# Routing of the second expert layer done batch by batch inside attention, into one DRAM bucket per expert

## The reference, cut to what matters

```
x = x + 0.5 * ffn(layernorm(x))
x = x + attention(layernorm(x))            # 16 heads of 8, causal softmax
x = x + 0.5 * ffn(layernorm(x))            # the same weights again

def ffn(inputs):                           # 8 experts, 128 -> 512 -> 128
    num = einsum('bsd,ed->bse', inputs, waff)
    aff = num / (|inputs| * |waff| + 1e-9)
    cap = floor(S * sigmoid(aff.mean() - threshold)), kept in 4..S   # mean over ALL tokens
    tcr = one_hot(argmax(softmax(aff)))    # each token's one expert
    ranks = argsort(argsort(-aff, axis=1)) # a token's rank within its batch, for each expert
    masks = tcr * (ranks < cap)
    out = sum over experts e of  gelu((inputs * masks[e]) @ W1[e] + b1[e]) @ W2[e] + b2[e]
```

## Time and profile before

| | us |
|---|---|
| median of 3 runs | 1154.74 |
| the profiled execution | 1151.91 |
| its span, first to last instruction | 1149.8 |
| busy PE / DVE / ACT / POOL | 910.6 / 707.3 / 592.5 / 719.7 |
| granted TensorE clock, mean | 0.877 |

### The profile page before, as it was taken

One profiled execution on the slowest core, in us unless ns is written; L12 is line 12 of the kernel. 1 busy time (PEld: TensorE's weight loads), 2 busy tenths in 40 slices (PEclk: granted clock), 3 DMA queues, 4 the chain that ended last, 5 costly groups with the idle time before them and its releaser, 6 DMA issues. The chain is left out here.

```text
span 1149.8 us, 25202 instructions
## 1 busy us (share of the span) xinstructions
PE 910.6 (79%) x8020; PEld 689.5 (60%) x8054; DVE 707.3 (62%) x2090; ACT 592.5 (52%) x1538; POOL 719.7 (63%) x1170
## 2 busy tenths in 40 slices
PE   2484638999936899999999999999883455988876
PEld 1383218999933566566666666666552225977876
DVE  6587944444416677777778777778654973433332
ACT  3023506666612666666666666666562423654543
POOL 4361976444132677777777777777552596777775
PEclk9655558999968999999999999999996556999998
DMA  5370002222216555555555665555510001212121
GB/s 165 88 191 20 1 9 65 69 67 68 51 47 118 104 104 113 118 117 106 111 108 109 122 116 102 112 113 111 106 27 10 1 1 41 52 52 52 48 50 30
DMA packets 124693, 89.01 MB, mean 77 GB/s; under 512 B 13649, under 2 KB 115078, under 8 KB 124566
## 3 DMA queue, kind: packets, MB, share of 16 engines
q1 hardware_dynamic: 101782, 52.36, 20.8%
q0 software_dynamic: 8960, 18.14, 6.9%
q10 hardware_dynamic: 13824, 16.92, 6.9%
HBM read 52.23 MB, written 34.87 MB: 76 GB/s over the span
## 5 line engine op out<-in xcount | busy, mean ns | idle before, releaser
L1341 DVE TENSOR_REDUCE at_mx<-at_pp 128x2 f32<-128x512 f32 (+1 forms) x384 | 260.4, 687 | 85.9 <-PE at_pp L1199 64.7
L1131 ACT ACTIVATE at_pt<-at_pm 128x512 f32<-128x512 f32 x384 | 224.6, 597 | 143.1 <-PE at_pm L1210 92.7
L1080 POOL TENSOR_SCALAR_AFFINE_SELECT at_pt<-at_pt 128x256 f32<-128x256 f32 (+1 forms) x384 | 182.1, 485 | 127.4 <-ACT at_pt L1131 123.1
L845 ACT ACTIVATE e_ht<-e_ps_h,b1t 128x128 f32<-128x128 f32 x576 | 164.5, 371 | 119.4 <-PE e_ps_h L873 119.2
L807 POOL DMA_INDIRECT e_x<-rows,gidx x144 | 138.6, 963 | 95.0 <-DVE e_y L925 49.1
L873 PE MATMUL e_ps_h<-e_xnt,e_w1own 128*128 128x128 f32 x1152 | 157.8, 281 | 25.5 <-issue 22.0
L873 PEld LDWEIGHTS e_ps_h<-e_xnt,e_w1own 128*128 128x128 f32 x1152 | 143.9, 197 | 29.5 <-issue 28.3
L883 PE MATMUL e_ps_y<-w,e_ht 128*128 x1152 | 160.1, 283 | 0.0
L883 PEld LDWEIGHTS e_ps_y<-w,e_ht 128*128 128x128 f32 x1152 | 140.8, 193 | 1.7
L925 DVE SCALAR_TENSOR_TENSOR e_y<-e_ps_y,e_x 128x256 f32<-128x256 f32 x72 | 30.5, 424 | 143.9 <-PE e_ps_y L883 143.9
L574 POOL TENSOR_SCALAR r_atp<-r_iotab,r_colp 128x128 bf16<-128x128 bf16 x128 | 91.5, 733 | 35.9 <-DVE r_colp L712 35.9
(11 more groups left out here) (256 smaller groups left out, 1622.7 us busy)
## 6 DMA issues: line engine op xcount, KB each, us to landing
at_qkd<-at_part SPq DMA_DIRECT2D x64, 192.0 KB, 3.0
kb<-at_qkd SPq DMA_DIRECT2D x64, 96.0 KB
qs<-at_qkd ACTq DMA_DIRECT2D x64, 96.0 KB
x<-e_y SPq DMA_DIRECT2D x36, 128.0 KB, 1.8
rows<-ts_x ACTq DMA_DIRECT2D x16, 264.0 KB, 3.1
rows<-at_x SPq DMA_DIRECT2D x32, 132.0 KB
ts_x<-in_x_dram SPq DMA_DIRECT2D x16, 256.0 KB, 3.2
x_by_token<-at_xa SPq DMA_DIRECT2D x32, 128.0 KB
```

The lines of the kernel that those rows point to most:

```text
L845: last = a.activation(hid_t[j % NB][:, f, :], ps_h[j % NB][:, f, :], ACT.Gelu, bias=c.b1t[:, ds(e, 1), f])
L1080: g.affine_select(out=tile, in_=tile, compare_op=ALU.is_ge, fill=0.0, base=0, pattern=[[0, n], [1, P]], channel_multiplier=-1).then_inc(ma ...
L1131: a.activation(pt[u % RING][:, :], pm[u % 2], ACT.Exp, scale=SCALE).then_inc(exped, 1)
L1341: v.tensor_reduce(out, src, axis=AX.X, op=ALU.max).then_inc(maxed, 1)
```

## The change

Stage r2 is gone. For the second layer, affinity, expert and rank are now computed per batch within `attention`, in a chain over turns b-2 and b-3:

- POOL (turn b-2, u = 1) puts the token's number into the row's last word. DVE turns size times norm into a reciprocal (u = 1, 2, 6), multiplies (u = 8), takes the maximum and the one-hot `hots` (u = 8 to 10); ACT and POOL split the affinity into three bf16 pieces (u = 8 to 11), and POOL adds up affinities and counts of earlier batches.
- One turn on (u = 0), PE transposes pieces and one-hots (4 matmuls) and with four more computes each token's place: expert times 66*128, plus tokens of earlier batches, plus tokens before it in this one. ACT copies the transposes out (u = 1), PE makes the comparisons (u = 3), DVE the ranks (u = 4, into the row's word RANK), POOL makes the place an integer (u = 4) and scatters the batch's 256 rows, by two indirect DMAs (u = 6, 7), into the DRAM table `buckets`, which has a bucket of 8448 rows for each expert.
- The row buffers `x2` are four and not two, `run` has one turn more (b up to 34), SP's DMA of the rows is gone, the PSUM tile `po` is one and not two (its place goes to `mr`), and PE's transpose of the maxima stands ahead of the projection at u = 8.
- A new stage `settle` after attention turns the counts of the buckets into each tile's expert and first row, fills the rows behind each bucket's end with blank rows (8 DMAs), and computes the capacity.
- In e2, SP loads each tile's 128 consecutive rows from its bucket by a plain DMA whose address comes from a register. POOL only scatters, by the token number in the row. The mask is rank <= limit, one DVE instruction.
- Small DVE instructions with one tensor input (`tensor_scalar`, `tensor_copy`) in token_stats and attention have become ones with two tensor inputs; a copy and an addition have become one addition. e1 and r1 are as before.

The diff, cut to its core:

```diff
@@ token_stats, attention: statistics, normalise
-                v.tensor_copy(vare[:, q, :, 1], x_row[k][:, :, D + 1])
-                v.tensor_scalar(vare[:, q, :, 0], x_row[k][:, :, D + 1], LN_EPS, None, ALU.add).then_inc(var_done, 1)
+                v.tensor_tensor(vare[:, q, :, :], x_row[k][:, :, D + 1:D + 2].to_broadcast([P, TS, 2]), c.eps[:, 0:TS, :],
+                                ALU.add).then_inc(var_done, 1)
-                    v.tensor_scalar(out[:, j, :], x[:, j, 0:D], x[:, j, D:D + 1], x[:, j, D + 1:D + 2],
-                                    ALU.subtract, ALU.mult).then_inc(done, 1)
+                    v.scalar_tensor_tensor(out[:, j, :], x[:, j, 0:D], x[:, j, D:D + 1],
+                                           x[:, j, D + 1:D + 2].to_broadcast([P, D]), ALU.subtract, ALU.mult).then_inc(done, 1)
@@ experts, POOL and SP
-                if not by_slot:
-                    pool.indirect_dma_start(y_dram, bass.IndirectOffsetOnAxis(ap=c.sidx[:, j:j + 1], axis=0),
+                for j in range(NS):
+                    s = (j // 2) % NR
+                    if j % 2 == 0:
+                        pool.wait_ge(y_done, j // 2 + 1)
+                    to = x_row[s][:, j % 2, TOKEN:TOKEN + 1].bitcast(I32)
+                    pool.indirect_dma_start(y_dram, bass.IndirectOffsetOnAxis(ap=to, axis=0),
                                             y_row[s][:, j % 2, :], None, bounds_check=T - 1, oob_is_err=False).then_inc(y_out[s], 16)
+                for j in range(NS):
+                    i, s = j // 2, (j // 2) % NR
+                    if j % IDS == 0:
+                        first = rows_of(sp, j)
+                    if j % 2 == 0:
+                        wait(sp, y_out[s], OUTS * (i // NR))
+                    sp.dma_start(x_row[s][:, j % 2, :], io["buckets"][ds(first[j % IDS], P), :]).then_inc(x_in[s], 16)
@@ attention, POOL
+                    if u in (6, 7) and has(-3):
+                        n, q, j = b - 3, (k - 3) % 2, u - 6
+                        wait(pool, ranked, n * TPB + (j + 1))
...
+                        pool.indirect_dma_start(io["buckets"], bass.IndirectOffsetOnAxis(ap=to[(k - 3) % NQ][:, j:j + 1], axis=0),
+                                                x2[(k - 3) % NQ][:, j, :], None).then_inc(row_out[(k - 3) % NQ], 16)
+                    if u == 11 and has(-2):
...
+                        wait(pool, hot_done, n + 1)
...
+                        g.tensor_tensor(upto, c.hots[q][:, 3 * TPB, :], c.hots[q][:, 0, :], ALU.add).then_inc(seen, 1)
...
+                        g.tensor_tensor(pieces[:, :, 2, :], rest_a[:, :, :], pieces[:, :, 1, :], ALU.subtract).then_inc(lo_done, 1)
@@ attention, ACT
+                    if u == 1 and has(-3):
+                        wait(act, spot_done, b - 2)
+                        wait(act, scored, b - 3)
+                        a.activation(as_rows[:, :], mr.bitcast(BF16)[0:3 * E, 0:2 * S], ACT.Copy).then_inc(turned_out, 1)
@@ attention, PE
+                    if u == 0 and has(-3):
+                        wait(pe, hot_done, b - 2)
+                        wait(pe, lo_done, b - 2)
...
+                                last = te.transpose(mr.bitcast(BF16)[0:3 * E, at:at + P], of[:, j, :], c.identb[:, :])
...
+                        te.matmul(spots, c.tri[:, :], c.hots[q][:, 0:3 * TPB:3, :], start=True, stop=False, skip_group_check=True)
...
+                    if u == 3 and has(-3):
+                        wait(pe, turned_out, b - 2)
+                        wait(pe, own_spot, b - 2)
+                        for j in range(TPB):
+                            last = te.matmul(mr[:, j * S:(j + 1) * S], as_rows[:, (TPB + j) * P:(TPB + j + 1) * P],
+                                             as_rows[:, 0:S], start=True, stop=True)
@@ attention, DVE
+                if u == 1:
+                    wait(dve, size_done, n + 1)
+                    v.tensor_tensor(den[:, :, :], wnorm_d[:, :].unsqueeze(1).to_broadcast([P, TPB, E]),
+                                    size[q][:, :].unsqueeze(2).to_broadcast([P, TPB, E]), ALU.mult).then_inc(den_done, 1)
+                if u == 2:
+                    wait(dve, turned_out, n + 1)
+                    v.tensor_tensor(spot[:, :, :], mr[:, S:S + TPB * E].rearrange("p (j e) -> p j e", e=E),
+                                    c.hots[q][:, 0:3 * TPB:3, :], ALU.mult).then_inc(own_spot, 1)
+                    for j in range(TPB if u == 4 and has(-3) else 0):
...
+                        v.scalar_tensor_tensor(beats[j][:, :], mr[:, j * S:(j + 1) * S], amax[q][:, j:j + 1], c.tie[:, j, :],
+                                               ALU.subtract, ALU.is_gt, accum_out=x2[(k - 3) % NQ][:, j, RANK:RANK + 1]).then_inc(ranked, 1)
@@ macaron
-        route(nc, m, c, "r2")
+        settle(nc, m, io, c)
```

More of the change, by code:

```diff
@@ L32 @@
 XW = D + 4
+RANK, TOKEN = D + 2, D + 3
+STRIDE = 66 * P
 H, HD = 16, 8
@@ L503, in consts @@
     c.place = m.sb("place", [P, NT], I32)
+    c.token = m.sb("token", [P, NT], I32)
+    c.blank = m.sb("blank", [P, XW])
+    c.hots = [m.sb(f"hots{k}", [P, 3 * TPB + 1, E], BF16) for k in range(2)]
+    c.aff_sum = m.sb("aff_sum", [P, TPB, E])
+    c.base = m.sb("base", [1, NSX], I32)
+    c.limit = m.sb("limit", [P, 1])
     return c
@@ L801, in experts_of, with rows_of @@
             return e
+        def rows_of(eng, j):
+            n = min(IDS, NS - j)
+            _, r = nc.values_load_multi_w_load_instructions(
+                c.base[0:1, j:j + n], engines=[eng.engine], min_val=0, max_val=E * STRIDE,
+                skip_runtime_bounds_check_because="a tile's first row is at most that of the blank rows behind the last bucket, E * STRIDE")
+            return r
         @blk.gpsimd
@@ L963, in attention @@
         SCALE = HD ** -0.5
-        xa, xr, x2 = two("xa", [P, TPB, D + 2]), two("xr", [P, TPB, D]), two("x2", [P, TPB, XW])
+        xa, xr, x2 = two("xa", [P, TPB, D + 2]), two("xr", [P, TPB, D]), [sb(f"x2{k}", [P, TPB, XW]) for k in range(NQ)]
         bn, vare = two("bn", [P, TPB, 6]), two("vare", [P, TPB])
@@ L998, in attention @@
         index = two("index", [P, TPB], I32)
-        NZ = 2 + 3
+        size, wnorm_d, tiny, far = two("size", [P, TPB]), sb("wnorm_d", [P, E]), sb("tiny", [P, TPB, E]), sb("far", [P, TPB, E], BF16)
+        den, aff, rest_a = sb("den", [P, TPB, E]), sb("aff", [P, TPB, E]), sb("rest_a", [P, TPB, E])
+        amax, wmax, weight = two("amax", [P, TPB]), sb("wmax", [P, TPB]), sb("weight", [P, TPB, E])
+        pieces, as_rows = sb("pieces", [P, TPB, 3, E], BF16), sb("as_rows", [3 * E, 2 * S], BF16)
+        spot, spot_of, beats = sb("spot", [P, TPB, E]), two("spot_of", [P, TPB]), two("beats", [P, S])
+        to = [sb(f"to{k}", [P, TPB], I32) for k in range(NQ)]
+        (size_done, den_done, rden_done, aff_done, summed, amax_done, hi_done, rested, mid_done, lo_done, weighed, wmax_done,
+         hot_done, seen, turned, turned_out, spot_done, own_spot, spot_got, scored, ranked, token_done, to_done, blanked, made) = (
+             sem(n) for n in (
+                 "size den rden aff summed amax hi rested mid lo weighed wmax hot seen turned turned_out spot own_spot "
+                 "spot_got scored ranked token to blanked made").split())
+        NZ = 3 + 2
+        NM = 5
         blk = ctx.enter_context(nc.Block())
@@ L1021, in run @@
         def run(turn):
-            for b in range(-4, B + 2):
+            for b in range(-4, B + 3):
                 turn(b, b % NQ, lambda o, b=b: 0 <= b + o < B)
@@ L1156, in turn @@
                                      mi[0][:, 0:TPB * D].rearrange("p (h d) -> p h d", d=HD), ACT.Copy).then_inc(v_out, 1)
-                    if u == 7 and has(-2):
-                        wait(act, num_mm, b - 1)
-                        a.activation(c.num[:, ds((b - 2) * TPB, TPB), :], mi[0][:, 0:TPB * E].rearrange("p (j e) -> p j e", e=E),
-                                     ACT.Copy).then_inc(num_out, 1)
                     if u == 7 and has(-1):
@@ L1276, in small @@
                         last.then_inc(ont_tr, 1)
+                    if u == 8 and has(1):
+                        wait(pe, mp_done, b + 2)
+                        wait(pe, v_out, b + 4, B)
+                        for j in range(TPB):
+                            last = te.transpose(mi[0].bitcast(BF16)[0:3 * H, j * P:(j + 1) * P],
+                                                mp[(k + 1) % 2][:, j, :, :].rearrange("p t h -> p (t h)"), c.identb[:, :])
+                        last.then_inc(mt_tr, 1)
                     if u == 8 and has(-1):
@@ L1282, in small @@
                         last.then_inc(proj_mm, 1)
-                    if u == 8 and has(1):
-                        wait(pe, mp_done, b + 2)
-                        wait(pe, v_out, b + 4, B)
-                        wait(pe, num_out, b - 1)
-                        for j in range(TPB):
-                            last = te.transpose(mi[0].bitcast(BF16)[0:3 * H, j * P:(j + 1) * P],
```

(2 more changed lines are left out.)

250 lines of the change are left out of this document (213 added, 37 removed).

## The result

The changed kernel took 1197.88 us (median of 4 runs, 1196.23 to 1202.38), the kernel before 1156.05 beside it: ratio 1.037, 95% interval 1.033 to 1.041. It is slower; the prediction was 1115 us and faster.

The account below looks back on a forecast made before the run. PE was taken to bound attention and e1, POOL's queue e2, and a DVE and POOL chain r2. 1151.9 - 1 - 30 - 51 + 42 = 1111.9, with the median 2.8 above: 1115 us, range 1086 to 1142.

Parts of the forecast that it names:

- The term for e2: In e2, loads move from POOL to SP and PE becomes the bound: -30 us, bounds 0 to -33.
- r2's replacement: Between attention and e2, 23 us of chain, barriers and settle replace 74.2 us: -51 us, bounds -57 to -42.
- `settle`: The new stage after attention, with DVE's dependent instructions, PE's row matmuls and blank DMAs: taken as 7 us.
- token_stats: One instruction less in 16 steps at 0.08: -1 us.
- the term for attention: 30 full turns, each +1.4 us longer: +42 us, bounds 9 (+0.3 a turn) to 81 (+2.7 a turn).
- what is queued behind the new waits?: In attention, POOL's later size delays DVE's normalising, so PE waits 0.6 us at u = 3.
- The +1.4: Each attention turn's growth: 1.1 us PE work plus 0.6 wait at u = 3, minus 0.3 given back.
- The 0.3 that I gave back at the key tile: PE's wait ahead of the key tile shrinks by 0.3 us, since the maxima's transpose stands 0.6 earlier.
- The jam: Rival: attention's in-order lists jam at POOL's mask 11 and the work behind it, turn +3.4 us, 1175 us; chance 0.12.
- The turn absorbs the work: Rival: attention's turn grows only +0.5 us, using PE's time not busy, 1088 us; chance 0.17.
- e2 keeps its pace: Rival: e2 keeps half or more of its old pace through register loads or scatters holding slots, 1135 us; chance 0.12.
- The contention of POOL and DVE through the two-input form of the normalisings: Rival: in attention they hold each other up in SBUF, +0.6 us a turn, +18, 1133 us; chance 0.12.

Follow-up runs that it names:

- a1: The changed kernel with POOL's three small instructions of u = 11 (two counts, third bf16 piece) ahead of mask 11: 1135.73 us, 0.982 of the kernel before.
- b4: The kernel before, with PE also waiting, behind its u = 0 transposes, for all masks of the previous batch: 1234.36 us, 1.0075 of the kernel before.
- c1: The kernel before, with PE also waiting, behind its u = 0 transposes, for POOL's deviations of batch b-2: 1257.88 us, 1.089 of the kernel before.
- c3: The same kernel as b3, run on the third chip: 1109.12 us, 0.959 of the kernel before.
- a4: The changed kernel with attention's four normalisings a turn back in their one-tensor-input form: 1200.23 us, 1.038 of the kernel before.
- a3_pe_late: The changed kernel with the work of turn b-3 one step later on all engines: 1148.01 us, 0.993 of the kernel before.
- b3: The changed kernel with a1's move, ACT's second DMA group at u = 11, DVE's size product two steps later, POOL's deviation before the second scatter: 1117.99 us.

## Why the prediction was wrong

**What held.** The term for e2 was -30 and came to -31.6, with results 4.0 us apart and PE full. For r2's replacement it was -51 (bounds -57 to -42) and came to -55.9; `settle` took 5.2 us from its first instruction on DVE to its last, not 7. token_stats: -0.6 for -1. POOL has 308.23 / 20.7 = 14.9 us a turn (15.1 without the issue gaps foretold), DVE 15.2 (14.7 foretold).

**What failed is the term for attention: +42 foretold, +131 measured** (602.6 - 471.9). Of the step "what is queued behind the new waits?" I followed one chain only, the size through DVE to PE's transposes at u = 3. That wait exists, 0.8 us, and is seen as soon as the other is gone (a1). But POOL's three small instructions behind mask 11 I charged only to the deviations that follow them, and not to PE, which needs the last of them at u = 0. The rows for it stood in the prediction: masks 11 and 0 run to 608.05, and PE, with its key tile at 605.83, goes on behind its transposes of u = 0 at 607.20 in the trace of before:

```profile
607.20 0.38 PE L1197 MATMUL at_pp<-kb,qs 96*128 96x512 bf16 x1
```

Mask 11 alone ends about 0.5 us after that (b4 measures it), and the three small ones take 0.65: 1.15 us could have been read from these rows. The new copy on ACT ahead of its DMA issues makes mask 11 later still: in the turn shown above it ends at 620.84, 1.2 us behind the time at which PE is ready. That is 2.1 us a turn in which PE, which bounds the stage, stands still.

**The second part of the failure is the clock.** I priced waits at their own length. 15.6 + 1.1 of work + 2.1 of wait is 18.8, and turns of 18.9 are there; most are 20.4, with 1.5 us from 3.5 us at half clock behind the wait. Over all turns the time lost to the lower clock is 51.7 us, against 5.7 before, so it is 46 of the 131. c1 shows both sorts of turn with the wait alone.

**The work itself** was priced about rightly: in c3, where moves have taken out the missed wait and the foretold one, a turn is 16.8 us, +1.2 against 15.6, and I had +1.1 for PE's instructions. The +1.4 was for a kernel with the foretold wait and without the missed one, and that is a1: 17.7 us, +2.1 (1.1, 0.8 at u = 3, 0.2 left at line 1353). The 0.3 that I gave back at the key tile does not show: PE's wait there is 0.6 us a turn in a1, 0.5 before. Attention is 69.6 us longer in a1 than before (541.5 - 471.9), inside the bounds of 9 to 81 but not 42. That the kernels with four and five moves take 1118.0, 1109.1 and 1102.4 us, near the 1115 foretold, is in part luck: the forecast was not for these orders.

**The rivals.** The jam (1175, 0.12) had the right sign and named mask 11, but its mechanism, POOL's and PE's work in a row that is too long for a turn, is refuted by a1: the same work, three instructions moved, -62 us. "The turn absorbs the work" and "e2 keeps its pace" are refuted by the rows above. The contention of POOL and DVE through the two-input form of the normalisings is refuted as a cause of the time by a4. The other small instructions with two inputs were not swapped back, so what their contention costs is not measured; of the waits of PE in the changed kernel, none of those in 430 to 850 is for the normalised rows at u = 3, which stand behind line 1466, the one that shows it most (last section). With 0.12 on the jam and a range that ended at 1142, I had treated the cost of waits in attention as bounded at +2.7 us a turn. This bound came from one chain and full clock, and neither was a bound.

**What stays open**: by how much the half-clock turns alone would be cheaper with a wait of 2 us but no fall of the clock; nothing that I ran parts these two, except that both sorts of turn occur side by side. Nor do the runs show why the clock falls behind one such wait and not behind the next.

## What to carry to other kernels

For every value that an added instruction hands to the engine that bounds the stage, write down the time at which that engine asks for it and what stands ahead of the producer in its in-order list, with the waits and DMA issues of a third engine that these depend on; one wait not followed decided this case. A wait of the matmul engine in the steady state has to be priced with the clock behind it: here a wait of 1.9 us cost its own length in 12 turns of c1 and 3.5 to 6.7 us in 14, while one of 0.5 us cost 0.4 in most turns of b4. And before a restructuring is judged slow, look whether its price is one wait that a move in a list takes away: this one went from 1.037 to 0.982 with one move, and to 0.951 with five.

## What the runs showed of the hardware

- A DVE instruction with two inputs in SBUF can be held beside a POOL instruction. The plainest case is line 1466 (128x16): in the 21 turns of 430 to 850 of the changed kernel it starts 0.05 or 0.17 us behind the start of a mask, takes 485 to 607 ns, mostly 605, and ends 0.03 us after the mask; in the last turn, with no POOL instruction beside it, it takes 0.17 us. The Trainium skill ("SBUF — State Buffer", "Who interferes with whom") states that a VectorE instruction with two inputs in SBUF contends with a GpSimd instruction that reads SBUF, and these rows agree. The masks themselves show nothing of it (414 and 415 ns): here DVE waits for POOL. One turn of the profile after:

```profile
625.21 0.63 POOL L1127 TENSOR_SCALAR_AFFINE_SELECT at_pt<-at_pt 128x512 f32<-128x512 f32 x1 [0.52 <-ACT at_pt L1210]
625.26 0.61 DVE L1466 TENSOR_TENSOR at_den<-at_den,at_tiny 128x16 f32<-128x16 f32 x1
```

- DVE's one-hot comparison (line 1454, two inputs in SBUF) takes 670 ns in the turns, where it starts 0.31 to 0.37 us into a POOL scatter and ends 0.04 us after it, and 0.21 us in the last turn (1012.65) beside a POOL addition. In a3_pe_late it starts 0.20 us into the scatter and takes 0.19 us. So not every scatter beside it holds it; what decides was not settled. This is read from the traces; no experiment changed only this, and what the 0.46 us cost the kernel was not measured. The rows of the profile after, a turn and the last one, and then a turn of a3_pe_late:

```profile
615.30 0.99 POOL L1158 DMA_INDIRECT buckets<-at_x,at_to  x1 [0.17 <-issue]
615.65 0.68 DVE L1454 TENSOR_TENSOR hots<-at_weight,at_wmax 128x48 bf16<-128x48 f32 x1
...
1012.65 0.21 DVE L1454 TENSOR_TENSOR hots<-at_weight,at_wmax 128x48 bf16<-128x48 f32 x1
1012.66 0.27 POOL L1166 TENSOR_TENSOR aff_sum<-aff_sum,at_aff 128x16 f32<-128x16 f32 x1
...
620.02 0.99 POOL L1158 DMA_INDIRECT buckets<-at_x,at_to  x1 [0.17 <-issue]
620.22 0.19 DVE L1454 TENSOR_TENSOR hots<-at_weight,at_wmax 128x48 bf16<-128x48 f32 x1
```

- On one chip of three the kernel before took 1225.5 us and not 1156. In the profile of b4_before_wait, from that chip, e2 has 795 PE instructions in 145 us, 6.6 us a unit where the earlier trace rows have 4.9, at a clock of 0.89:

```profile
1055.00:1200.00 145.00, 113.83 (x795) 104.84 (x796) 39.37 (x132) 57.34 (x202) 88.84 (x89) 0.89 0.17 41
```

  The kernels whose rows come by SP's plain loads kept 4.0 to 4.1 us a unit on that chip (b3: 1146 instructions in 130 us). In that stretch of b4 PE is busy 113.83 us, part of it at the lower clock, and POOL, whose queue ran without a pause in the earlier trace rows, waits 31.4 us (11 times) for DVE's results. That results and queue hold each other back there is a reading of these waits; where it begins, and why on this chip and not on the others, was not settled.
